# Graph attention on one core: one source column in 48 fetched row by row from SyncE instead of gathered by GpSimd

## The reference

```
h = relu(layernorm(x))
for l in range(3):
    f   = leaky_relu((nf @ W_ni)[src] + (nf @ W_nj)[dst] + ef @ W_fij + bias, 0.2)   # E x 4 x 32
    e   = einsum('ehd,hd->eh', f, attn)                                              # E x 4
    a   = softmax of e over the edges with the same dst
    nf' = segment_sum((nf @ W_node)[src] * a, dst)
    nf, ef = nf'.mean(heads), f.mean(heads)
return x + nf
```

## Time and profile before

| | us |
|---|---|
| median of three runs | 3382.18 |
| the profiled execution, its own time | 3382.53 |
| its span, first to last instruction | 3380.7 |
| TensorE busy (matmul) | 2677.5 (79%) |
| VectorE busy | 2183.4 (65%) |
| ScalarE busy | 1648.5 (49%) |
| GpSimd busy | 2459.0 (73%) |
| chain that ended last: GpSimd, TensorE, issue, DMA | 51%, 19%, 18%, 7% |
| TensorE's granted clock in nearly the whole span | 0.50 |

### The profile page before, as it was taken

How to read it: one execution, slowest core, us unless ns; L and a number is a source line. 1 busy time by engine, 2 the same in 40 slices (tenths; PEclk the granted TensorE clock), 3 DMA queues, 4 the chain that set the end, 5 groups by cost and what they waited for, 6 DMA issues and landing times.

```text
span 3380.7 us, 34349 instructions
## 1 busy us (share of the span) xinstructions
PE 2677.5 (79%) x8858; PEld 1997.1 (59%) x8858; DVE 2183.4 (65%) x5325; ACT 1648.5 (49%) x3374; POOL 2459.0 (73%) x2595
## 2 busy tenths in 40 slices
PE   2299988888887288888888988827888888888883
PEld 1177766666665256666666666625666666666663
DVE  5288876767676247667676766624766767676663
ACT  0166655555555045555555555513555555555541
POOL 5777777777775777777777777667777777777773
PEclk8655555555555555555555555555555555555555
DMA  6143433333322323333323233232233232322222
GB/s 226 50 132 108 138 107 112 103 117 104 117 80 105 97 74 108 110 107 107 123 95 122 95 107 101 84 102 83 85 102 100 85 104 95 103 90 85 87 75 80
DMA packets 131212, 346.73 MB, mean 103 GB/s; under 512 B 48232, under 2 KB 88682, under 8 KB 111444
## 3 DMA queue, kind: packets, MB, share of 16 engines
q1 hardware_dynamic: 45492, 282.83, 22.3%
q0 software_dynamic: 82688, 46.77, 8.7%
q10 hardware_dynamic: 2838, 14.94, 1.1%
HBM read 131.12 MB, written 213.25 MB: 102 GB/s over the span
## 4 chain that ended last, share of the span: by engine, by line
POOL 51%; PE 19%; issue 18%; DMA 7%; DVE 4%; ACT 1%; POOLq 0%; DVEq 0%; ACTq 0%
POOL rows L453 49%; PE f_ps L567 7%; PE f_ps L575 7%; DMA rows<-nf_tab,src_sb 5%; PE xT_ps L557 4%; POOL edge_first L464 2%; DVE U L1070 1%; DMA U<-fix_tab 1%; POOL z L507 1%; DVE lr L1004 1%; DVE U L906 1%; PE wide_ps L639 1%; ACT f_low L686 0%; ACT up L731 0%; PE xT_ps L627 0%
## 5 line engine op out<-in xcount | busy, mean ns | idle before, releaser
L453 POOL DMA_INDIRECT rows<-nf_tab,src_sb x2424 | 2288.3, 944 | 761.6 <-issue 728.7
L575 PEld LDWEIGHTS f_ps<-w_out,lr 128*128 128x128 f32 x4848 | 1167.5, 331 | 622.4 <-issue 577.7
L567 PE MATMUL f_ps<-xT,w_edge 97*128 97x512 f32 x1212 | 1157.3, 1057 | 10.4 <-ACT xT L678 10.4
L557 PE MATMUL xT_ps<-ident,rows 128*97 128x128 f32 x2424 | 692.0, 439 | 502.2 <-DMA rows<-nf_tab,src_sb 352.1
L575 PE MATMUL f_ps<-w_out,lr 128*128 128x36 f32 (+1 forms) x4848 | 1052.8, 371 | 17.9 <-DVE lr L1004 17.8
L1004 DVE TENSOR_TENSOR lr<-f_ps,f_low 128x512 f32<-128x512 f32 x606 | 416.3, 687 | 890.5 <-ACT f_low L686 886.5
L557 PEld LDWEIGHTS xT_ps<-ident,rows 128*97 128x97 f32 x2424 | 518.2, 279 | 558.4 <-DMA rows<-nf_tab,src_sb 350.0
L1070 DVE TENSOR_TENSOR_SCAN U<-wide_ps,U 128x272 f32<-128x272 f32 (+1 forms) x1224 | 797.9, 715 | 1.2 <-ACT wide_ps L720 0.7
L678 ACT ACTIVATE xT<-xT_ps 97x512 f32<-97x512 f32 x606 | 357.7, 590 | 396.0 <-PE xT_ps L557 390.8
L686 ACT ACTIVATE f_low<-f_ps 128x512 f32<-128x512 f32 x606 | 360.6, 595 | 336.4 <-PE f_ps L567 334.7
L720 ACT ACTIVATE wide_ps<-e_dec 128x289 f32<-128x289 f32 (+1 forms) x612 | 403.4, 676 | 161.8 <-DVE U L1070 158.9
(11 more groups left out here) (135 smaller groups left out, 615.5 us busy)
## 6 DMA issues: line engine op xcount, KB each, us to landing
u_tab<-up SPq DMA_DIRECT2D x150, 1088.0 KB, 4.2
rows<-nf_tab,src_sb POOLq DMA_INDIRECT x2424, 2.4
first_st<-edge_first SPq DMA_DIRECT2D x48, 768.0 KB, 6.0
ef_tab<-ef_new SPq DMA_DIRECT2D x32, 768.0 KB, 4.2
ef_st<-ef_tab SPq DMA_DIRECT2D x32, 768.0 KB
edge_first<-first_st ACTq DMA_DIRECT2D x16, 768.0 KB, 12.1
ef_st<-in_edge_attr_dram SPq DMA_DIRECT2D x16, 672.0 KB
U<-fix_tab SPq DMA_DIRECT2D x3, 1062.5 KB
```

Source lines behind the costliest of these rows:

```text
L453: eng.indirect_dma_start(rows[q % RING][:, c * K:c * K + D], None, nf_tab[:, :], bass.IndirectOffsetOnAxis(ap=src_sb[:, t:t + 1], axis=0)) ...
L557: mm = eng.transpose(xT_ps[y][0:K, u * P:(u + 1) * P], rows3[q % RING][:, a * GT + u, :], ident[:, :])
L567: eng.matmul(f_ps[n % 3][:, :], w_edge[l][:, :], xT[y][0:K, :], start=True, stop=True).then_inc(f_ready, 1)
L575: mm = eng.matmul(f_ps[n % 3][:, u * m:(u + 1) * m], lr[y][:, u * P:(u + 1) * P], w_out[l][:, 0:m], start=True, stop=True)
```

## The change

Of each super block but the last of a layer, column 47 is no longer gathered. Its 128 rows are fetched by SyncE in 128 plain DMAs of 128 bytes. Their node numbers stand in a new small tile `one_idx`, one partition for each super block, loaded once at the start by two DMAs of single numbers. SyncE loads 8 numbers into registers at once (`REGS = 8`), then, for each row, makes the address in the table (one instruction) and starts the DMA (one instruction). TensorE's `turn` waits in addition on `one_rows` in the group that holds column 47. The fetch for super block s+1 stands in step s of SyncE's list, cut into as many pieces as there are result stores in the step and put behind each: 40, 40 and 48 rows, or all 128 behind the only store of step 0. Those of a layer's first super block stand at the layer's start, 64 before the first two `first_st` loads and 64 behind them.

```diff
+        NONE = NS - 1
+        def by_sp(t):
+            return t % SUP == SUP - 1 and t // SUP < NONE
+        def gathered(g):
+            return sum(not by_sp(g * GT + u) for u in range(GT))
+        def rows_sem_to(q, a):
+            return 16 * sum(gathered((v % NS) * GS + a) for v in range(q % RING, q + 1, RING)
+                            if (v % NS) * GS + a < NG)
+        def ones_to(q):
+            return 16 * P * sum(v % NS < NONE for v in range(q % RING, q + 1, RING))
...
+                def fetch_ones(q, p0, p1):
+                    if q % NS >= NONE:
+                        return
+                    if p0 == 0 and q >= RING:
+                        eng.wait_ge(prod_done, (q - RING + 1) * SUBS)
+                    c = SUP - 1
+                    for p in range(p0, p1, REGS):
+                        _, at = nc.values_load_multi_w_load_instructions(
+                            one_idx[q % NS:q % NS + 1, p:p + REGS], engines=[SP_ENGINE],
+                            min_val=0, max_val=N - 1,
...
+                        for u, row in enumerate(at):
+                            eng.dma_start(rows[q % RING][p + u:p + u + 1, c * K:c * K + D],
+                                          nf_tab[bass.ds(row, 1), :]
+                                          ).then_inc(one_rows[q % RING], 16)
...
+                eng.dma_start(one_idx[0:NONE, 0:FULL],
+                              src2[:, 0:NONE * SUP].rearrange("p (s c) -> s c p", c=SUP)
+                              [:, SUP - 1, :],
+                              allow_slow_non_contiguous=True).then_inc(one_in, 16)
+                eng.dma_start(one_idx[0:REST1, FULL:P], ...
                 eng.wait_ge(nf_ready, NPART)
                 store_nf()
...
                 for l in range(L):
                     q0, k0 = l * NS, l * NB
+                    if l == 0:
+                        eng.wait_ge(one_in, 32)
+                    eng.wait_ge(tab_out, (l + 1) * 16)
+                    fetch_ones(q0, 0, P // 2)
                     load_first(q0)
                     load_first(q0 + 1)
+                    fetch_ones(q0, P // 2, P)
                     for s in range(NS):
...
-                        for b in range(max(SUBS * s - 2, 0), SUBS * s + 1):
+                        mine = range(max(SUBS * s - 2, 0), SUBS * s + 1)
+                        for i, b in enumerate(mine):
                             store_u(k0 + b)
+                            if s + 1 < NS:
+                                cut_p = [P * a // len(mine) // REGS * REGS
+                                         for a in (i, i + 1)]
+                                fetch_ones(q0 + s + 1, cut_p[0],
+                                           P if i == len(mine) - 1 else cut_p[1])
...
                 def gather_cols(l, cols):
                     for t in cols:
+                        if by_sp(t):
+                            continue
...
-                        eng.wait_ge(src_rows[q % RING][a], visits(q, a) * 16 * GT)
+                        eng.wait_ge(src_rows[q % RING][a], rows_sem_to(q, a))
+                        if gathered(g) < GT:
+                            eng.wait_ge(one_rows[q % RING], ones_to(q))
```

More of the change, by code:

```diff
@@ L10 @@
 ACT = mybir.ActivationFunctionType
+SP_ENGINE = mybir.EngineType.SP
 AX = mybir.AxisListType
@@ L28 @@
 SLOPE = 0.2
+REGS = 8
 def egat_kernel(nc, x, src, dst, edge_attr, W_ni, W_nj, W_fij, W_node, attn, bias, out):
@@ L120, in egat_kernel @@
         src_sb = sb("src_sb", [P, T], I32)
+        one_idx = sb("one_idx", [NS, P], I32)
         same = sb("same", [P, T])
@@ L211, in egat_kernel @@
         src_rows = [[sem(f"src_rows{s}_{a}") for a in range(GS)] for s in range(RING)]
+        one_in = sem("one_in")
+        one_rows = [sem(f"one_rows{s}") for s in range(RING)]
         ef_in = [sem(f"ef_in{s}") for s in range(2)]
@@ L279, in ef_in_count @@
             return 16 * sum(ef_loads(a) for a in range(q % 2, q + 1, 2))
-        def visits(q, a):
-            return sum((v % NS) * GS + a < NG for v in range(q % RING, q + 1, RING))
+        NONE = NS - 1
+        REST1 = max((REST - SUP) // SUP + 1, 0)
+        def by_sp(t):
[7 more added lines that the diff above has]
+            return 16 * P * sum(v % NS < NONE for v in range(q % RING, q + 1, RING))
         def carry_of(u, w):
@@ L337, in store_ef @@
                                   ).then_inc(ef_out[q % 2], 16)
+                def fetch_ones(q, p0, p1):
[8 more added lines that the diff above has]
+                            min_val=0, max_val=N - 1,
+                            skip_runtime_bounds_check_because="src holds node numbers below N")
+                        for u, row in enumerate(at):
+                            eng.dma_start(rows[q % RING][p + u:p + u + 1, c * K:c * K + D],
+                                          nf_tab[bass.ds(row, 1), :]
+                                          ).then_inc(one_rows[q % RING], 16)
                 def store_u(k):
@@ L361, in _ @@
                               src[FULL * T:E].rearrange("(p t) -> p t", p=1)).then_inc(src_in, 16)
+                eng.dma_start(one_idx[0:NONE, 0:FULL],
+                              src2[:, 0:NONE * SUP].rearrange("p (s c) -> s c p", c=SUP)
+                              [:, SUP - 1, :],
+                              allow_slow_non_contiguous=True).then_inc(one_in, 16)
+                eng.dma_start(one_idx[0:REST1, FULL:P],
+                              src[FULL * T:FULL * T + REST1 * SUP]
+                              .rearrange("(s c) -> s c", c=SUP)[:, SUP - 1:SUP],
+                              allow_slow_non_contiguous=True).then_inc(one_in, 16)
                 eng.wait_ge(nf_ready, NPART)
```

1 line of the change is left out of this document (added).

## The result

The changed kernel takes 4066.74 us (median of four runs, 4065.88 to 4070.48), the kernel before 3382.21 on the same chip: 1.2025 times as long, 95% interval 1.2007 to 1.2043. Forecast were 4150 us, in a range of 3320 to 4950, with a chance of 0.78 for slower.

The account below looks back on a forecast made before the run. GpSimd's gathers bound the kernel; without 47 of them SyncE's row fetches become the bound. Layers lose 289.8 + 242.3 + 236.0 = 768 us, so 3382.5 + 768 = 4150 us, range 3320 to 4950.

Parts of the forecast that it names:

- c: SyncE's time for one fetched row: DMA 0.38, address 0.08, share of register load 0.10, together 0.56 us.
- GpSimd's gathers bound the kernel before; SyncE was free: Before the change: gathers on the end's path, 47 removed worth 58.5 us; SyncE busy 3.9 us in 50 to 60.
- F: SyncE's time for one super block's 128 fetched rows, 128 x c: 71.9 us, ends 47 and 242.
- The two times that the prediction works out for other loads: Whole kernel, if the Trainium skill's register load prices hold: 4780 at 200 ns a register, 4060 at a 600 ns floor.
- 46 us for each us of F: All layers together: the kernel's time moves 46 us for each us of F.
- Layer one: First layer's last transpose begins at 293.5 + 15F, 1372.0 instead of 1082.2: +289.8 us.
- The start of layers two and three: First 64 rows ahead of the `first_st` loads delay each layer's start by F/2 - 14.9 = 21 us.
- The steps of layers two and three: SyncE's other issues add 2.6 us a step in layer two, 2.2 in three; layers lose 242.3 and 236.0.
- What waits behind SyncE's work: Result stores queued behind SyncE's rows: pieces of 22 to 27 us against 34 that `lay_out` can wait; only step 0 hurts.
- TensorE's stall: At its transposes in group 11: waits for a row DMA once in a super block, some 25 us long.
- SyncE keeps up: Rival at SyncE's fetches: c under 0.40 in layer one, 0.43 elsewhere, all 47 gathers count, 3324 us; chance 0.19 for faster.
- The row DMAs back up: Rival at SyncE's queue: 128 rows fill it, c = 1.22, about 8020 us; c above 0.70 has chance 0.18, this included.

Follow-up runs that it names:

- e1b_static: Changed kernel with each row DMA reading a fixed table row, no register load or address instruction: 3326.6 us, 0.9836 of the kernel before.
- e4b_regs16: Changed kernel with 16 registers to a load instead of 8: 3944.45 us, 1.1664 of the kernel before.
- e5_behind: Changed kernel with all 128 rows of a layer's first super block behind the two `first_st` loads: 4094.79 us, 1.2087 of the kernel before.
- e6_onepiece: Changed kernel with a fetch's 128 rows in one piece behind a step's third result store: 4432.9 us, 1.3084 of the kernel before.
- t2_eight: Changed kernel with SyncE fetching only every second super block, 24 rows behind each result store, GpSimd gathering the rest: 3356.21 us, 0.9923 of the kernel before.

## Why the prediction was right

The bound, the place and the sign were right, and the time was 83 us too high, in a loss of 685 (12%). It came so near in part by luck: the parts of c were off against each other, and in layer two so were two mistakes of the sum.

- **GpSimd's gathers bound the kernel before; SyncE was free.** Right: e1b_static takes 55.6 us off by skipping 47 gathers on the path, forecast 58.5.
- **F.** Forecast c = 0.56 and F = 71.9; the trace gives 0.54. From the first store's end, 184.6, to the last row of the first layer, 1291.8, are 1107.2 us; less 14 x 3.9 and divided by 15, F is 70.2. (128 x 0.54 are 69; the rest is loads that stand directly behind a store.) The parts were off against each other. The DMA with its gap is 0.228 + 0.05, not 0.38: I had taken L321's mean, with its three slow first issues, where its usual length was nearer. The address costs 0.037, and the MOVE 0.029, which wasn't counted, and two more gaps: 0.16 together, not 0.08. The load, the least sure term (between 0.25 and 2.4), was taken as 0.75 and has a median of 0.79. The two times that the prediction works out for other loads should be 4780 and 4040: the second stands there as 4060, but 16 x 0.15 x 46 = 110 us less than 4150 are 4040.
- **46 us for each us of F.** Right in kind: 1.7 us less in F are 78 us of the 83. e4b_regs16 gave 122 us for 2.4 to 3 us, 41 to 51 for each.
- **Layer one:** 293.5 + 15 x 70.2 = 1346.5, measured 1349.1.
- **The start of layers two and three** failed. The step was that 64 rows ahead of `first_st` delay the layer by F/2 - 14.9 = 21 us. The load is late by 22.1, as said, but the first store is only 3.7 late. Two things make up for the rest. GpSimd went on gathering meanwhile, so that TensorE found its groups ready where before it had waited for gathers. And TensorE's granted clock, 0.50 (its level of 1.2 GHz) nearly everywhere, was 1.00 (2.4 GHz) in that stretch. It had stood idle for 51.5 us until `first_st` came; soon after it began, its transposes came 2.17 us apart instead of 4.2, until the clock was back at 0.50 at 1500. Before, and in e5_behind, it had stood idle for 29 us, and from 1200 on (in e5_behind from its start) the clock was 0.50. From the first transpose of layer two to that of group 12 are 35.1 us (1474.26 to 1509.33) and were 55.6 (1184.70 to 1240.32). Twelve groups at the half clock with nothing to wait for take 50.5, so by this estimate the ready gathers gave back 5 us and the clock 15. Layer three is alike: 51.0 us idle, then 1.00 from 2810 to 2823. The changed kernel's two rows stand first, then one of the kernel before:

```profile
1474.26 1.99 PE L614 MATMUL xT_ps<-ident,rows 128*97 128x128 f32 x8 [51.49 <-DVE rows L1052]
core 0: us, PE busy (x) PEld busy (x) DVE busy (x) ACT busy (x) POOL busy (x), PEclk, DMA share, GB/s
1484.00:1490.00 6.00, 5.99 (x42) 4.67 (x41) 3.99 (x16) 4.93 (x12) 4.48 (x6) 1.00 0.10 17
1210.00:1220.00 10.00, 8.86 (x28) 6.51 (x28) 3.94 (x18) 4.45 (x11) 7.54 (x8) 0.50 0.09 15
```

- **The steps of layers two and three.** In layer two another mistake hid this one. A step takes 74.3 us, as the last two rows below show, where F = 70.2 and the 2.6 us of other issues make 72.8. The load of `ef_st` takes 0.86 us for the 0.53 taken, and the register load behind the step's first store 1.7 to 1.8 where it is 1.05 to 1.25 in layer one. In 14 steps that is 21 us, as much as the start was overpaid, and layer two loses 221 where the sum with F = 70.2 gives 216. In layer three a step takes 72.8 (3421.04 to 3493.86), near the 72.4 of the sum; nothing hides the mistake there, and 197 stand against 210. (The first row below is where the fetches of layer one end.)

```profile
1291.87 0.36 SPq L353 DMA_DIRECT2D ef_tab<-ef_new  x1
...
2027.73 0.36 SPq L353 DMA_DIRECT2D ef_tab<-ef_new  x1
2102.04 0.36 SPq L353 DMA_DIRECT2D ef_tab<-ef_new  x1
```

- **What waits behind SyncE's work.** I wrote that only step 0 hurts ScalarE. It is wrong: ScalarE waited 555.1 us for stores, in 122 of 153 places, 4.5 us each. TensorE's stall of 74.0 - 50.5 = 23.5 us in a super block, forecast in one piece of 25, stands to 12.7 us (569.3 / 45) at group 11 and for most of the rest at its edge multiplies, behind ScalarE (9.5 us in the step shown). It added nothing to the sum here, since SyncE never waited for it, but e6_onepiece shows it turn into 366 us when the stores are bunched.
- **SyncE keeps up** (chance 0.19) didn't happen here. Its condition was c under 0.40, and e1b_static, with 0.335 a row, shows it to be right; t2_eight keeps up at c = 0.54 with half of the rows. **The row DMAs back up** fell: 0.228 us in the median, 0.931 at most.

## What to carry to other kernels

An engine that only issues transfers looks free in a profile that counts busy time. Before giving it work, count its instructions for each piece of work, one gap for each, and set the sum against the period of the loop: here 0.54 us a row made 70 us in a slot of 59, and a change that could gain 58 us at most lost 685. Where a helper engine is too slow for all of the work, give it the share that its rate allows, well below the bound, and in small pieces between the things others wait for. And a delay at the start of a stage is not a delay of the stage: the supplier that bounds it goes on meanwhile, and an engine that has stood idle may start at a higher granted clock. Look at both before moving the whole stage.

## What the runs showed of the hardware

- SyncE's instruction with a register address costs no more than one with a fixed address: 0.228 us against 0.252 in the median (the changed kernel and e1b_static). What costs is around it: the address 37 ns, a MOVE 29 ns, gaps of about 45 ns, the load.
- A load of registers from SBUF is 0.33 us and 0.058 for each register; directly behind a store of 1 MB it takes 0.9 to 1.8 us with 8 registers and 1.4 to 3.9 with 16, 3.0 in the median.
- TensorE's granted clock went from 0.50 (1.2 GHz) to 1.00 (2.4 GHz) where it had stood idle for 51 us and then found its work ready (1484 to 1496 us), and back to 0.50 by 1500. After 29 us idle and work that came by and by, it was at 0.50 (e5_behind, 1475 to 1540).
- On one chip SyncE had pauses of about 0.7 us between instructions, the other engines idled for causes without a name, and the kernel before took 4007 instead of 3382 us. The kernels with register addresses suffered most: the one with 16 registers to a load has a ratio of 1.36 there and 1.17 elsewhere, the one without registers 1.006 and 0.984. On SyncE an address instruction of 37 ns was up to 1410 ns long there. The cause was not looked for.

```profile
L369 SPq FUSED_REGOPS  x6144: 1/37/1410, 99.8 to 5308.4; - x199
```
